# A four-layer graph network on one core: zero fills of a scatter table issued four tiles earlier, and an edge-softmax preparation moved up two tiles

## The reference

```python
edge_index = jnp.stack([src, dst])
x = _layernorm(x + _L0_gnn_ref(x, edge_index, edge_weight, ...))   # segment_sum of weighted messages
x = _layernorm(x + _L1_gnn_ref(x, edge_index, edge_type_2, ...))   # twice rgcn_gate_layer, relu between
x = _layernorm(x + _L2_gnn_ref(x, edge_index, ...))
x = _layernorm(x + _L3_gnn_ref(x, edge_index, edge_attr_8, ...))

def rgcn_gate_layer(x, row, col, edge_type, basis, att, gate_w, root, bias):
    w = jnp.einsum('rb,bio->rio', att, basis)          # 2 relations from 30 bases of 512 x 512
    x_j = x[col]
    for r in range(2):
        gate = sigmoid(x_j @ gate_w[r, :, 0]);  msgs.append(gate[:, None] * x_j @ w[r])
    agg = segment_sum(where(edge_type == 0, msgs[0], msgs[1]), row)
    return agg + x @ root + bias

# layer 3: logits get att_bias[e, h]; softmax over the edges of a row
logits = einsum('ehd,ehd->eh', q[rows] * scale, k[cols]) + att_bias
p = exp(logits - row_max[rows]);  att = p / segment_sum(p, rows)[rows]
```

## Time and profile before

| | us |
|---|---|
| median of 3 runs (1331.4 to 1337.19) | 1332.22 |
| the profiled execution | 1337.19 |
| its span, first to last instruction | 1335.3 |
| TensorE busy | 1229.6 (92%) |
| VectorE busy | 857.0 (64%) |
| ScalarE busy | 419.5 (31%) |
| GpSimd busy | 303.9 (23%) |
| mean granted TensorE clock | 0.976 |
| the 39 fills L701, bytes each | 1280 KB, median 11.2 us to landing |
| `z_high` L1317 on ACT, `z_low` L922 on DVE, mean of one | 0.687, 0.750 |

### The profile page before, as it was taken

One profiled execution on the slowest core, in us unless ns is written; L12 is line 12 of the kernel. 1 busy time (PEld: TensorE's weight loads), 2 busy tenths in 40 slices (PEclk: granted clock), 3 DMA queues, 4 the chain that ended last, 5 costly groups with the idle time before them and its releaser, 6 DMA issues.

```text
span 1335.3 us, 22146 instructions
## 1 busy us (share of the span) xinstructions
PE 1229.6 (92%) x8447; PEld 551.9 (41%) x8448; DVE 857.0 (64%) x1174; ACT 419.5 (31%) x564; POOL 303.9 (23%) x220
## 2 busy tenths in 40 slices
PE   6888888699998999999999999989999999999996
PEld 2233333233343333344454543443333555555552
DVE  7476666144434555452478773748999887978876
ACT  2445555322232112212301002135541343433431
POOL 2011110000100232344555655555640000000000
PEclk9989999799998999999999999999999999999998
DMA  8678887697695787744122221112322655545552
GB/s 316 242 271 274 261 263 232 259 365 295 213 371 187 265 279 260 252 118 122 17 33 35 47 65 2 2 12 32 41 42 96 222 196 184 195 166 178 177 167 77
DMA packets 65099, 228.02 MB, mean 171 GB/s; under 512 B 31272, under 2 KB 36136, under 8 KB 48790
## 3 DMA queue, kind: packets, MB, share of 16 engines
q1 hardware_dynamic: 35192, 159.02, 34.9%
q0 software_dynamic: 25184, 53.10, 15.4%
q10 hardware_dynamic: 4638, 14.69, 3.1%
HBM read 201.56 MB, written 62.56 MB: 198 GB/s over the span
## 4 chain that ended last, share of the span: by engine, by line
PE 44%; DVE 10%; issue 7%; DMA 5%; ACT 1%; SPq 0%; DVEq 0%
PE PS L1657 17%; PE PS L1632 6%; PE PS L1902 4%; DMA R<-in_basis_s 4%; DVE R L1084 4%; PE PS L1889 4%; PE PS L1919 3%; DVE R L1119 3%; PE PS L1784 2%; PE PS L1908 2%; PE PS L1496 2%; DVE R L1135 1%; PE PS L1699 1%; PE PS L1603 1%; DMA W<-w_d 1%
## 5 line engine op out<-in xcount | busy, mean ns | idle before, releaser
L734 POOL DMA_INDIRECT bias_d<-R x160 | 266.2, 1664 | 346.7 <-DMA bias_d<-R 229.0
L1657 PE MATMUL PS<-R 128*128 128x512 f16 x1300 | 297.2, 381 | 11.4 <-DMA R<-sup_d 9.8
L1657 PEld LDWEIGHTS PS<-R 128*128 128x128 f16 x1300 | 121.2, 98 | 193.4 <-issue 59.1
L1560 PE MATMUL PS<-R,XX 125*128 125x512 f16 (+2 forms) x612 | 131.0, 347 | 26.2 <-DVE R L848 17.6
L1460 ACT ACTIVATE R<-PS 128x1024 f32<-128x1024 f32 (+1 forms) x100 | 100.4, 1005 | 166.6 <-PE PS L1889 166.6
L1632 PE MATMUL PS<-W,XX 128*128 128x512 f16 x600 | 139.4, 393 | 5.6 <-DMA W<-w_d 2.9
L1119 DVE SCALAR_TENSOR_TENSOR R<-R,W 128x1024 f32<-128x1024 f32 (+1 forms) x68 | 133.5, 1992 | 7.1 <-ACT R L1460 6.0
L1084 DVE CUSTOM_DVE_ANT_0 R<-PS,R 128x1250 f16<-128x1250 f32 x80 | 116.8, 1459 | 5.5 <-PE PS L1836 2.9
L848 DVE TENSOR_SCALAR R<-W,R 125x1250 f16<-125x1250 f16 x160 | 89.4, 605 | 47.3 <-PE PS L1560 43.5
L1902 PE MATMUL PS<-R 128*32 128x256 f32 (+1 forms) x1600 | 105.9, 382 | 5.4 <-DVE R L1119 4.8
L1889 PE MATMUL PS<-R 128*128 128x256 f16 (+3 forms) x800 | 107.3, 277 | 1.7 <-DVE R L1084 1.1
(11 more groups left out here) (215 smaller groups left out, 1361.4 us busy)
## 6 DMA issues: line engine op xcount, KB each, us to landing
bias_d<-bias_d POOLq DMA_DIRECT2D x39, 1280.0 KB, 11.2
R<-in_basis_s SPq DMA_DIRECT2D x48, 1024.0 KB, 6.5
W<-bias_d SPq DMA_DIRECT2D x27, 1024.0 KB, 4.9
R<-bias_d SPq DMA_DIRECT2D x13, 1024.0 KB, 4.9
W<-in_basis_s SPq DMA_DIRECT2D x12, 1024.0 KB, 6.3
R<-key_d SPq DMA_DIRECT2D x20, 500.0 KB, 3.8
R<-R SPq DMA_DIRECT2D x120, 80.0 KB, 6.1
W<-bias_d SPq DMA_DIRECT2D x7, 904.0 KB, 4.5
```

What stands on the lines that cost most here:

```text
L734: pool.indirect_dma_start(bias_d, bass.IndirectOffsetOnAxis(ap=idx[:, c:c + 1], axis=0), attr[:, c, :], None, bounds_check=DUMP + GC * P - ...
L1560: ins = T.matmul(mm_out(3 * (j % 2) + b, p1 - p0), own[0:EC, bass.ds(c, 1), :, :].rearrange("p c m w -> p (c m w)"), hots(p0, p1), start=f ...
L1657: ins = T.matmul(mm_out(4 + i % 2, D), lhs, rhs, start=n == 0, stop=n == len(terms) - 1)
```

## The change

Two things are moved; nothing is computed differently.

1. POOL: eight of the 40 fills are issued in pairs when 4, 5, 6 and 7 tiles of layer 0 are out. Before, one went at 8 and one at 9. The last group, after tile 10 and the mixed weights, has five fills in place of eleven.
2. In the stage of `z_tile(1, k)`: the keys from k = 4 to k = 2, the maximum and the index array from k = 5 to k = 3, the two small PE steps from after tiles 6 and 8 to after 4 and 6, DVE's reduction between them from k = 7 to k = 5 (behind the split of the root weight, which stays), the subtraction and the exponential from k = 9 to k = 7.

```diff
--- before.py
+++ after.py
@@ -712,12 +712,13 @@
                 pool.wait_ge(built, 4 * k + 3)
                 for n in range(ZE + ZB * k // ZK, ZE + ZB * (k + 1) // ZK):
                     zeros(n)
-            for k in range(2):
-                pool.wait_ge(o_done, NT - 2 + k)
-                zeros(ZE + ZB + k)
+            for k in range(4):
+                pool.wait_ge(o_done, 4 + k)
+                for n in range(ZE + ZB + 2 * k, ZE + ZB + 2 * k + 2):
+                    zeros(n)
             pool.wait_ge(o_done, NT)
             pool.wait_ge(w_in[0], 16 * 4)
-            for n in range(ZE + ZB + 2, ZF):
+            for n in range(ZE + ZB + 8, ZF):
                 zeros(n)
             pool.iota(bramp, [[-1, GC * EC]], base=GC * EC, channel_multiplier=0,
                       allow_small_or_imprecise_dtypes=True).then_inc(bramp_made, 1)
@@ -935,7 +936,7 @@
             turned_low(1, NT - 1)
             for k in range(1, NT):
                 z_low(1, k)
-                if k == 4:
+                if k == 2:
                     dve.wait_ge(b_in, 16 * 5)
                     V.tensor_copy(bdf[0:HALF, :, :], bdst_c[0:HALF, :, :])
                     step(V.tensor_copy(bsf[0:HALF, :, :], bsrc_c[0:HALF, :, :]))
@@ -945,7 +946,7 @@
                     step(V.tensor_copy(btf[0:EC, :], bsrc_t[0:EC, :]))
                     V.scalar_tensor_tensor(bkey[0:EC, :], bkey[0:EC, :], float(NN), btf[0:EC, :],
                                            ALU.mult, ALU.add).then_inc(bkey_made, 1)
-                if k == 5:
+                if k == 3:
                     V.tensor_reduce(bmax[0:EC, :], attr[0:EC, :, :].rearrange("p c h -> p h c"), AX.X,
                                     ALU.max).then_inc(bmax_made, 1)
                     for e in range(GC):
@@ -957,12 +958,11 @@
                                        own_dump.rearrange("p (u i) -> p u i", u=1).broadcast_to([P, CH // GC, GC])))
                 if k == 5:
                     split_low(0)
-                if k == 7:
                     dve.wait_ge(bmt_done, 1)
                     step(V.tensor_reduce(bmax1[0:HEADS, :], mm_out(7, EC, HEADS), AX.X, ALU.max))
                     V.tensor_scalar(diag8[0:HEADS, :], ident[0:HEADS, 0:HEADS], bmax1[0:HEADS, :], None,
                                     ALU.mult).then_inc(bdiag_made, 1)
-                if k == 9:
+                if k == 7:
                     dve.wait_ge(bmb_done, 1)
                     V.tensor_tensor(attr[0:EC, :, :], attr[0:EC, :, :],
                                     PS[0:EC, 6, 0:HEADS].rearrange("p (u h) -> p u h", u=1).broadcast_to(
@@ -1681,10 +1681,10 @@
             gates(0, NT - 1)
             for k in range(2, NT):
                 z_tile(1, k)
-                if k == 6:
+                if k == 4:
                     pe.wait_ge(bmax_made, 1)
                     T.transpose(mm_out(7, EC, HEADS), bmax[0:EC, :], ident[0:EC, 0:EC]).then_inc(bmt_done, 1)
-                if k == 8:
+                if k == 6:
                     pe.wait_ge(bdiag_made, 1)
                     T.matmul(mm_out(6, HEADS, EC), ones[0:HEADS, 0:EC], diag8[0:HEADS, :], start=True,
                              stop=True).then_inc(bmb_done, 1)
```

## The result

The changed kernel takes 1347.05 us (median of 4 runs, 1345.55 to 1350.23), the kernel before 1331.81 (4 runs, 1326.12 to 1337.19): a ratio of 1.0118 [1.0073, 1.0165], 15.2 us. A second set of runs of the same two kernels gave 1346.83 against 1329.53, 1.0118 [1.0092, 1.0144]. (The ratios are not formed from the two medians, so the two differ by up to 0.15%: 1.0118 is 15.7 us.) I had forecast 1338.0, 5.8 us slower, with "within 0.5%" as likeliest. The sign was right; the loss is two and a half times the forecast, and the time stands at the very end of my range of 1329 to 1347.

The account below looks back on a forecast made before the run. TensorE, busy nine tenths, was taken as the bound. Fills + 15.0, first z tile - 3.8, z stage moves - 3.05 and - 2.35 gave + 5.8 on the median 1332.2, so 1338, with 8 in 10 for 1329 to 1347.

Parts of the forecast that it names:

- within 0.5%: Whole kernel: time within about 6.7 us of no change, given 0.46, against 0.10 for faster and 0.44 for slower.
- the one on the keys: z stage, keys at k = 2: edge loads land about 373, k = 2 done near 383, so no gain or loss.
- Fills in tiles 4 to 7: Layer 0's output: four added pairs, 27.2 us of every engine, cost 15.0 us, 13.3 of stops and 1.7 of clock.
- cover: Tiles 4 to 7: 6.0 us of idle DMA time plus a slab's 6.2 us lead, 12.2 together, absorb fill time.
- halves behind stores: Tiles 4 to 7: PE stops naming ACT or DVE would show the forecast wrong the other way.
- upper end: Fills in tiles 4 to 7: 22.9 us, with 3.96 a fill, two clock falls and late `w_d` stores counted in.
- First z tile: End of layer 0: mixed weights' load in time without the old fills, gaining 1.94 and the clock's 1.83, together 3.8 us.
- The z stage's own moves: z stage: gain 3.05 us at tile 7's stop and 2.35 at the stop ahead of the output stage.
- The clock: TensorE: stops from about 1.7 to 1.9 us up also cost clock, 1.83, 1.79 and 1.60 us at three stops.
- One to one turns: DMA queues in tiles 4 to 7: packets alternate, judged likelier than whole-packet draining because a 78 KB store took 21.2 us.
- The third: Rival on tiles 4 to 7: fills at 3.96 us each, stores held back, 13.7 us slower, 1346; 28 in 100.

## Why the prediction was wrong

**The step that failed** is the one on the keys: "Ten us of slack, so nothing." It took 10.7 us as what the loads need, when it was what they need with a lead of 2 to 5 us over the fills. That lead came from a wait, POOL's for the mixed weights, and I had just argued that wait away, for 3.8 us of gain. Gain and loss have one cause, and I entered only the gain. The row to price it with was there: a store of 78 KB took 21.2 us beside fills, 10.5 more than I reckoned for these loads, and the slack was ten. Beside the fills they took 25.4, and without any 5.2. Measured in the z stage: 6.31 of stop and 1.33 of clock, 7.6 us; the z stage fell by just these when the group was held back. With it, 5.8 + 7.6 is 13.4. The fills' 16.9 in place of 15.0 make it 15.3, beside 14.45 in the stages of the two profiles and 15.2 in the medians. Agreement to a tenth is chance: the two profiles themselves lie 11.8 apart, and a clock fall more or less is 1.6 to 1.8.

**Fills in tiles 4 to 7: size nearly right, by two errors.** Stage 14.94 longer although its last stop of 1.94 went, so 16.9. By the rows it is 14.4 of stops and 3.0 of clock behind them, 0.6 of a stop at 293.39 that comes before any fill, less 1.2 of clock that before lost in its first output tile and this execution did not. But three pairs cost all of it, where I had 8.2; the fourth, for which I had put 5.1, cost nothing: from 345 to 358 us PE was busy for 13.00 of 13. The 20.0 us of the three pairs had a cover of 5.6, not 12.2. The 6.2 of a slab's lead was not to be had in full. That the stores come due first is only a part of it: with a third buffer the stops were still 9.85 of 10.96. I had named the stores ("halves behind stores") as the way to be wrong and left them in the upper end, giving ACT 5 us that a store of 14 us does not leave.

**First z tile.** As forecast in size: 1.94 and 1.70 of clock (1.83) gone. The cause was named too narrowly. The load of the mixed weights lands in 6.2 us in place of 7.1; more comes from the stores before it, from whose first issue to the load's it took 6.1 us before (344.35 to 350.46) and 3.1 now (359.41 to 362.50).

**The z stage's own moves.** Right. Forecast 5.4 (3.05 and 2.35). With the moves alone the z stage is 3.90 shorter and the ten matmuls behind it 1.60 (2.32 in place of 3.92), 5.5 in the rows; the time says 4.2, with 2.5 to 6.1 by its interval. Stops 0.37 in place of the forecast 1.0, a new one of 0.53 (forecast 0.5 to 0.6), 1.66 (forecast 1.65). Of the 5.5 some 1.7 is luck, since the fills alone, with the old stop of 2.26, had full rate behind it too.

**The clock.** "Somewhere near 1.7 to 1.9 us a stop begins to cost its clock too" is refuted in both directions: 0.72 and 1.26 were followed by slow rows, 2.26 (the fills alone), 3.24 and 3.92 by full ones.

**One to one turns.** Borne out between loads and fills: 18 packets beside 18 in the changed kernel, 362 beside 361 with short rows. I had carried them over to a store of 78 KB; for the stores of `w_d` no run decides it.

**The rivals.** The third (more per fill, stores held back, 1346) came nearest by its sum and in half of its mechanism: the stores, yes; 3.96 a fill, no (3.33). It too had no stop in the z stage.

## What to carry to other kernels

When a stop is taken away, list everything that it held back, and place each again against what runs there then: a group of transfers that used to start behind a late load now starts beside the next loads. Slack read from a landing time holds only with the neighbours that the transfer had in that trace. A bulk fill in DRAM that nobody waits for still takes time on the DMA engines, 3.33 us of every one of them for a fill here, so it does not belong where the queues are already full. Its row length is worth a try before its place: cutting 40 KB packets to 4 KB gave 3.9 us on the moves alone and about 17 on the changed kernel, while no other place that was tried for the fills gained anything clear of noise. And look in the program for what stands behind a wait: here the next stores did.

## What the hardware showed that I had not expected

- A load of 640 KB took 5.2 us with no fill beside it, 10.1 to 10.7 with eleven fills of 1.3 MB issued about 2 us behind it, 25.4 with five issued 2.5 us ahead of it, and 13.2 with five in packets of 4 KB, 2.3 us ahead.
- The granted clock does not follow the length of the last stop. The same 24 matmuls took 7.04 us behind stops of 0.72 and 1.26, and 5.34 or 5.35 behind none, 0.52 or 0.53; 48 took 10.52 behind 2.26 in one profile, and 12.21 behind 2.26 in another. Two profiles of the same kernel (the changed one) gave a second-layer z stage of 56.99 and 55.30 us. A term of 1.6 to 1.8 us for a clock fall is thus as much a matter of chance as of the change, in a forecast of this kernel.
- Loads and fills shared the engines packet by packet at both sizes tried: 18 and 18 with fills of 40 KB (0.74 MB against 0.14 in 2 us), 362 and 361 with 4 KB (1.41 MB against 2.68 in 10 us). So the size of the fill's packets sets how many bytes of load pass meanwhile.
- Four stores issued at 339.55 to 340.88 behind two fills had their first packet only after 343 us. A count over a stretch in which a queue has nothing ready (20 packets beside 549) tells nothing of how two queues share.
